# Moving the second layer's cross-attention values out of the decoder's inner loop

## The reference

```python
q = x @ Wq.T + bq                 # 128 x 128, per sequence
k = context @ Wk.T + bk           # 77 x 128
v = context @ Wv.T + bv           # 77 x 128
p = softmax(heads(q) @ heads(k).T)          # 16 heads, each row sums to 1
x = layernorm(x + (p @ heads(v)) @ Wo.T + bo)
```

## Time and profile before

| | us |
|---|---|
| median of 3 runs (lowest, highest) | 801.29 (800.78, 802.55) |
| the profiled execution | 800.58 |
| its span, from first to last instruction | 798.8 |
| busy in the span: PE, PEld, DVE | 662.6, 502.5, 585.7 |
| busy in the span: ACT, POOL | 408.7, 207.4 |
| layer 2, from 478.6 to the end | 320.2 |
| layer 2's loop in its steady part, 516.0 to 750.2 | 234.2 |
| of that PE busy, DVE busy, ACT busy | 212.01, 193.02, 132.25 |

### The profile page before, as it was taken

How to read it: one execution, slowest core, us unless ns; L and a number is a source line. 1 busy time by engine, 2 the same in 40 slices (tenths; PEclk the granted TensorE clock), 3 DMA queues, 4 the chain that set the end, 5 groups by cost and what they waited for, 6 DMA issues and landing times.

```text
span 798.8 us, 20635 instructions
## 1 busy us (share of the span) xinstructions
PE 662.6 (83%) x8166; PEld 502.5 (63%) x8166; DVE 585.7 (73%) x1639; ACT 408.7 (51%) x1172; POOL 207.4 (26%) x212
## 2 busy tenths in 40 slices
PE   5767999999999698998652967889898999989973
PEld 3345777777777476777531965666666666666641
DVE  1346888888888889896746475788888887888743
ACT  3656666666666355664210222465555555565532
POOL 5211233333333311423425042222222222222100
PEclk9969999999999889999955896999999999999975
DMA  9666534445444424450022110000000001100000
GB/s 356 241 198 212 180 124 156 158 164 176 158 159 156 155 57 160 145 213 12 25 86 68 36 39 14 10 12 11 12 12 12 16 12 16 14 12 12 5 5 7
DMA packets 48255, 72.18 MB, mean 90 GB/s; under 512 B 2832, under 2 KB 43280, under 8 KB 45472
## 3 DMA queue, kind: packets, MB, share of 16 engines
q1 hardware_dynamic: 45120, 61.80, 23.0%
q0 software_dynamic: 2320, 5.18, 3.0%
q10 hardware_dynamic: 720, 3.88, 1.2%
HBM read 32.38 MB, written 38.47 MB: 89 GB/s over the span
## 4 chain that ended last, share of the span: by engine, by line
PE 48%; DVE 30%; issue 12%; ACT 6%; DMA 2%; POOL 0%; SPq 0%; DVEq 0%; POOLq 0%; ACTq 0%
PE bank L490 40%; PE bank L542 4%; DVE sc L1172 3%; PE bank L625 3%; DVE nmxa L1176 2%; DVE k L1506 2%; DVE scol L1548 1%; ACT kbd L1094 1%; ACT kbd L1095 1%; DVE q L1226 1%; DVE nmb L1231 1%; DVE k L1484 1%; DVE q L1575 1%; DMA xT_ld<-xT 1%; DVE y_d L1522 1%
## 5 line engine op out<-in xcount | busy, mean ns | idle before, releaser
L431 POOL TENSOR_TENSOR early<-early,recb 128x616 f32<-128x616 f32 x32 | 38.9, 1216 | 212.1 <-DVE recb L1262 212.1
L951 ACT ACTIVATE sc<-sc,nmxa 128x128 f32<-128x128 f32 x256 | 78.1, 389 | 9.6 <-DVE nmxa L1176 9.6
L1506 DVE TENSOR_TENSOR k<-bank,k_sb 128x512 f32<-128x512 f32 x64 | 41.1, 684 | 30.7 <-PE bank L490 20.1
L1172 DVE TENSOR_TENSOR sc<-bank,rel 128x512 f32<-128x512 f32 x64 | 41.1, 683 | 19.1 <-PE bank L490 19.1
L490 PE MATMUL bank<-k,xdT 128*128 128x512 f32 x96 | 49.1, 651 | 0.0
L1184 DVE COPY pTa<-bank 128x512 f32<-128x512 f32 x32 | 21.9, 691 | 33.7 <-PE bank L542 33.6
L490 PE MATMUL bank<-pTb,v 77*32 77x128 f32 x1024 | 37.3, 284 | 10.8 <-DVE pTb L1269 4.9
L408 POOL TENSOR_TENSOR rext<-rext,ones 128x1008 f32<-128x1008 f32 x16 | 29.9, 1868 | 60.3 <-ACT rext L936 60.3
L467 POOL TENSOR_TENSOR oTb<-x_all,row_sb 128x128 f32<-128x128 f32 x16 | 7.6, 478 | 142.9 <-DVE pTa L1527 135.5
L936 ACT ACTIVATE rext<-bank 128x512 f32<-128x512 f32 x64 | 34.8, 608 | 18.1 <-PE bank L490 18.1
L490 PE MATMUL bank<-kbd 32*128 32x256 f32 x256 | 38.1, 417 | 5.3 <-DVE kbd L1500 4.6
(11 more groups left out here) (269 smaller groups left out, 1812.6 us busy)
## 6 DMA issues: line engine op xcount, KB each, us to landing
rel_dram<-rext SPq DMA_DIRECT2D x16, 2040.0 KB, 7.1
rel<-rel_dram SPq DMA_DIRECT2D x16, 960.0 KB, 5.6
rext<-w_up SPq DMA_DIRECT2D x1, 1792.0 KB, 8.3
rel<-w_down SPq DMA_DIRECT2D x1, 1792.0 KB, 8.8
wb<-w_b ACTq DMA_DIRECT2D x1, 1604.0 KB, 16.7
xT_ld<-xT SPq DMA_DIRECT2D x16, 64.0 KB, 7.0
x_all<-x ACTq DMA_DIRECT2D x1, 1024.0 KB, 11.8
rel<-rel_dram SPq DMA_DIRECT2D x16, 64.0 KB, 5.7
```

What stands on the lines that cost most here:

```text
L431: G.tensor_tensor(pB[:, part, :], pB[:, part, :], recb[:, part].unsqueeze(2).broadcast_to([P, 8, C]), ALU.mult).then_inc(b_even, 1)
L951: last = A.activation(sc[:, h, :], sc[:, h, :], ACT.Exp, bias=nmxa[:, h:h + 1])
L1172: added = mark(V.tensor_tensor(sc[:, part[i], :], bank[2 * j + i][:].rearrange("p (a j) -> p a j", a=4), rel[:, t % 2, part[i], :], ALU.add))
L1506: V.tensor_tensor(scd[:, 4 * i:4 * i + 4, :], bank[(1, 2, 0, 1)[i]][:].rearrange("p (a t) -> p a t", a=4), const("causal").unsqueeze(1).br ...
```

## The change

- `v1` leaves both lists of the loop, TensorE's and VectorE's. Between the layers, behind the keys, TensorE makes the values of all 16 sequences into banks 3, 6, 4 and 7, and ScalarE copies them to places in SBUF that are free from then on (seven copies: three of four sequences, four of one).
- A new `v1` on ScalarE copies a sequence's values, SBUF to SBUF, into `ve`, two rounds ahead, between `e_q` and `f_ln`. `e_v` waits for it instead of `e_s`.
- The bias isn't added to the values. VectorE scales the output weights by it (`wo_bv`), TensorE sums that over the features with `ones`, in front of the product with `wabs`, and VectorE adds the row to `c1_bo`.
- The lists are written anew. Read around the ring, the differences are these. TensorE: `e_q` is in front of `f_down` instead of behind it. VectorE: `f_norm` goes from behind `f_i4` to behind `f_clamp`, a round's half later; `c_s1` is in front of `f_q0`; `f_q1`, `f_q2` and `f_q4` are in front of `c_ag`; `f_q3` is in front of `c_norm`; `d_r0` and `d_r1` change places. GpSimd: `d_res` of a sequence runs one round later, in the same place behind `e_res`.

The diff, cut to its core:

```diff
@@ -83,15 +83,15 @@
 ORDER2 = {
-    "pe": ("v1 f_turn:-2 e_out:-1 d_qk:1 e_x d_gv:1 f_down:-2 e_q d_rank:1 f_x:-1 e_s f_up:-1 e_nm d_s01:1 "
-            "e_st d_s3:1 e_inj d_v:1 d_out:1 e_v d_x:2").split(),
-    "dve": ("f_clamp:-1 d_m2:1 d_m3:1 f_silu:-1 c_s0:2 f_q0:-1 c_s1:2 c_st:2 c_ag:2 f_q1:-1 d_add:1 f_q2:-1 "
-            "d_st:1 d_ag:1 c_norm:2 f_q3:-1 f_q4:-1 d_n0:1 d_n1:1 D_st:1 D_ag:1 e_div v1:1 d_norm:1 e_add e_st "
-            "e_ag d_r1:2 e_norm d_r0:2 f_i0 d_rope:2 f_i1 f_add:-1 f_i2 f_st:-1 f_i3 f_ag:-1 f_i4 f_norm:-1 "
-            "d_gate:2 d_q:2 e_m0:1 e_m1:1 e_m2:1 e_m3:1 d_k:2 d_m0:2 d_m1:2").split(),
-    "act": ("e_e2 d_v:1 e_e3 c_ln:2 d_ln:1 e_v d_x:2 d_ln2:1 f_turn:-1 e_ln e_x:1 d_gates:2 e_q:1 f_ln:-1 f_x "
-            "d_sig:2 e_nm:1 f_exp f_sig e_e0:1 e_e1:1").split(),
-    "pool": "gather:2 e_res d_res:2 d_fade:2".split(),
+    "pe": ("d_gv:1 e_q f_down:-2 d_rank:1 f_x:-1 e_s f_up:-1 e_nm d_s01:1 e_st d_s3:1 e_inj d_v:1 d_out:1 e_v "
+            "d_x:2 f_turn:-1 e_out d_qk:2 e_x:1").split(),
+    "dve": ("f_i4:-1 d_gate:1 d_q:1 e_m0 e_m1 e_m2 e_m3 d_k:1 d_m0:1 d_m1:1 f_clamp:-1 f_norm:-2 d_m2:1 d_m3:1 "
+            "f_silu:-1 c_s0:2 c_s1:2 f_q0:-1 c_st:2 f_q1:-1 f_q2:-1 f_q4:-1 c_ag:2 d_add:1 d_st:1 d_ag:1 "
+            "f_q3:-1 c_norm:2 d_n0:1 d_n1:1 D_st:1 D_ag:1 e_div d_norm:1 e_add e_st e_ag d_r0:2 e_norm d_r1:2 "
+            "f_i0 d_rope:2 f_i1 f_add:-1 f_i2 f_st:-1 f_i3 f_ag:-1").split(),
+    "act": ("e_e2 d_v:1 e_e3 c_ln:2 d_ln:1 e_v d_x:2 d_ln2:1 f_turn:-1 e_ln e_x:1 d_gates:2 e_q:1 v1:2 f_ln:-1 "
+            "f_x d_sig:2 e_nm:1 f_exp f_sig e_e0:1 e_e1:1").split(),
+    "pool": "e_res:-1 d_res d_fade:1 gather:2".split(),
     "sp": "f_store:2".split(),
...
@@ -100,6 +100,10 @@
                         "d_r1", "d_rope", "d_rank"), 1)
+V1_BANKS = (3, 6, 4, 7)
...
@@ -248,6 +253,11 @@
         ve, vd = va[0:2], va[2]
+        cflat = cT[:, :, :].rearrange("p b j -> p (b j)")
+        values4 = [cflat[0:C, 0:4 * P], cflat[0:C, 4 * P:8 * P], xT_ld[0:C, :, :].rearrange("p n d -> p (n d)")]
+        values1 = [cflat[0:C, 8 * P:9 * P], y["a"][0:C, :], y["b"][0:C, :], q[2][0:C, :]]
+        v1_sb = [values4[t // 4][:, t % 4 * P:(t % 4 + 1) * P] for t in range(12)] + values1
         nme, nmTe = nmb, nmT
...
@@ -726,14 +736,24 @@
                 mm(bank[i][:, 0:(hi - lo) * C], w("c1_wk"), flat[:, lo * C:hi * C]).then_inc(k0_ps, 1)
+            pe.wait_ge(b_pT_dve, 2 * B)
+            for t in range(B):
+                last = mm(bank[V1_BANKS[t // 4]][0:C, t % 4 * P:(t % 4 + 1) * P], cT[:, t, :], w("c1_wv"))
+                if t % 4 == 3:
+                    last.then_inc(v_ps, 1)
             for n in range(2 * E):
                     pe.wait_ge(k0_sb, 3 * XC + 3)
+                if n == 12:
+                    pe.wait_ge(v_lo, B + 1)
                 last = pe.transpose(bank[n // 4][:, n % 4 * P:(n % 4 + 1) * P], xg[:, n, :], ident)
             pe.wait_ge(w_sum, 1)
+            pe.wait_ge(v_lo, B + 7)
+            mm(bank[7][:, P:2 * P], ones[:], wo_bv[:])
             mm(bank[7][:, 0:2], ones[:], wabs[:]).then_inc(w_mean, 1)
...
@@ -828,7 +848,6 @@
                 need(pe, var["e"], t)
-                pe.wait_ge(v_hi, B + t + 1)
                 for i in range(4):
...
@@ -849,16 +868,13 @@
                 pe.wait_ge(exped["b"], 4 * (B + t) + 4)
+                pe.wait_ge(v_hi, B + t + 1)
                 head_products(bank[3], ve[t % 2], pTe, C)
                 mm(bank[4][:, 0:P], oTe, w("c1_wo")).then_inc(proj["e"], 1)
-            def v1(t):
-                pe.wait_ge(exped["b"], 4 * (B + t))
-                mm(bank[5][0:C, 0:P], cT[:, t, :], w("c1_wv")).then_inc(v_ps, 1)
...
@@ -1052,6 +1068,13 @@
+            for n in range(3):
+                act.wait_ge(v_ps, 2 * B + 4)
+                A.activation(values4[n], bank[V1_BANKS[n]][0:C, :], ACT.Copy).then_inc(v_lo, 1)
+            for n in range(4):
+                A.activation(values1[n], bank[V1_BANKS[3]][0:C, n * P:(n + 1) * P], ACT.Copy).then_inc(v_lo, 1)
             def m_turn(i):
...
@@ -1066,6 +1089,10 @@
                 A.activation(yg[:, n, :], bank[3][:, 0:P], ACT.Copy).then_inc(m_y_act, 1)
+            def v1(t):
+                need(act, values["e"], t - 1)
+                A.activation(heads(ve[t % 2][:])[0:C], by_head(v1_sb[t]), ACT.Copy).then_inc(v_hi, 1)
...
@@ -1410,6 +1437,7 @@
             dve.wait_ge(ld_wf, 16)
+            step(V.tensor_scalar(wo_bv[:], w("c1_wo"), col("c1_bv"), None, ALU.mult))
             step(V.tensor_reduce(wabs[:, 0:1], fw[:, 0:HID], AX.X, ALU.add, apply_absolute_value=True))
...
@@ -1430,6 +1458,7 @@
                 dve.wait_ge(w_mean, 1)
+                V.tensor_tensor(row("c1_bo"), bank[7][:, P:2 * P], row("c1_bo"), ALU.add)
                 V.tensor_scalar(wmean[:], bank[7][:, 0:2], 1.0 / (P * HID), 1e-5, ALU.mult, ALU.max).then_inc(w_ready, 1)
...
@@ -1530,11 +1559,6 @@
                 add("e", 4, lambda t: xe)(t)
-            def v1(t):
-                dve.wait_ge(v_ps, 2 * B + t + 1)
-                V.tensor_tensor(heads(ve[t % 2][:])[0:C], by_head(bank[5][0:C, 0:P]), by_head(row("c1_bv")[0:C, :]),
-                                ALU.add).then_inc(v_hi, 1)
```

33 lines of the change are left out of this document (17 added, 16 removed).

## The result

The changed kernel took 804.22 us (median of 9 runs, 802.87 to 808.02), the kernel before 801.29 (9 runs beside it, 800.78 to 803.36). The ratio is 1.0037, with a 95% interval from 1.0021 to 1.0052: slower by 2.9 us. The forecast was 803.6, with a range of 799.8 to 806.2. Two executions, one of 1101.42 us (kernel before) and one of 1582.3 us (last kernel of the experiments), ran in a far slower state and are left out of every median and ratio.

What follows compares the result with a forecast made beforehand. Each 18.02 us round was bound by TensorE from `d_rank` to the mask, then by VectorE's pace; 0.15 x 13 = 1.95, plus 0.3 between the layers and 0.1 drain, +2.35 on 801.29: 803.6, range 799.8 to 806.2.

Steps and rivals of the forecast that it cites:

- The rule for adding up: On VectorE, an independent follower starts duration - 0.08 later, a dependent one 0.03 after the end; `c_st` to `d_n0` 2.07, +0.11.
- `f_norm`: Moved behind `f_clamp` into VectorE's half of the round: +0.04 per round, at most +0.11, at least 0.
- The sum for the loop: Layer 2's 13 rounds, each longer by 0.04 (`f_norm`) + 0.11 (`f_q` steps) = 0.15: 1.95 us.
- `v1` leaves VectorE: In front of `d_norm`, which waits for ScalarE anyway, removing the 0.28 us step gains 0.00 per round.
- The case of fewer steps: Rival: VectorE's step count sets the second half's pace, `v1` gives 0.20 in 16 rounds: 798.4 us; chance 0.16.
- `v1` enters ScalarE: A copy of about 0.3 between `e_q` and `f_ln`, where ScalarE waits 0.97 for VectorE: 0.00.
- `v1` leaves TensorE: Its 0.38 pair goes, but `e_out` waits 0.32 for VectorE's division, which is late next: 0.00.
- The rival of the clock: Layer 2's start: the hole left by `v1` delays TensorE's clock rise, +1.2 to +3.5, 804.8 to 807.1; chance 0.11.
- GpSimd's sums: Rival: `d_res`, ending 643.3, meets `f_clamp` at 643.41 and holds it 0.2 in 13 rounds: +2.6, 806.2; chance 0.06.
- Between the layers: The product with `ones` comes when TensorE has no slack left: +0.3 (0.2 to 0.6); the values and copies cost 0.
- My sign of being wrong: Wrong if the round is shorter than 18.02, or the stages before 478 us differ by over 1 us.
- The drain: Last rounds, `e_q` in front of `f_down`, where VectorE has less to do ahead of `f_add`: 0.1 once.

Runs made afterwards that it cites:

- last kernel of the experiments: Kernel before with `f_clamp` in front of `d_m0`, `f_exp`, `f_q4`, `f_q1` moved, and `d_v`'s ScalarE copy and GpSimd's gather earlier: 801.79 us beside 802.17, 0.9991.
- the first experiment: Changed kernel with the kernel before's lists, their `v1` taken out (values between the layers, ScalarE's `v1` kept): 801.81 us, 1.0021 to the kernel before.

## Why the prediction was right, and where it wasn't

**The rule for adding up** held. It gave 2.07 for `c_st` to `d_n0`; measured 2.05. The term was +0.11 for a round; the run with the `f_q` steps alone gives 18.10 - 17.99 = +0.11.

**`f_norm`** was +0.04 and is +0.01 (2.99 against 2.98), and the run with it alone shows no longer round. In after `f_silu` starts 647.83 - 646.05 = 1.78 behind `f_clamp`, not 1.81: the step takes 646.63 - 646.38 = 0.25 and not 0.27, and the masks behind it 1.20 and not 1.21. And the earlier trace rows leave `f_silu` a slack of 0.24 and not only the idle 0.16 that I counted with. The sum for the loop, 1.95, should have been 13 x 0.12 = 1.56; the profiled one shows 1.17, because before has one round of 18.31. A single round that is 0.3 longer stands at the same place, the third, in all traces of kernels with `v1` on VectorE (with `f_clamp` alone, in the first three; the two kernels built on that one have a further long round later), and in none with `v1` on ScalarE; of those only the one without the bias row has a longer round, the fifth. The kernel with the product kept on TensorE has none, so the product isn't the cause. Why it is the third round isn't known.

**`v1` leaves VectorE: 0.00.** Right, and shown by the first experiment: `d_norm`'s wait is 0.42, forecast 0.43 to 0.5. The case of fewer steps (798.4) was wrong for this reason.

**`v1` enters ScalarE: 0.00.** Right in the round (17.99 with the old lists). ScalarE's wait in front of `f_ln` shrank from 0.97 to 0.79.

**`v1` leaves TensorE: 0.00 per round**, right for the round, wrong at the start. This is the step of the prediction that failed in the profiled execution: the sum has nothing for the start, and it measured 31.42 against 29.66, +1.76. The rival of the clock, to which I had given 0.11, has the size in its +1.2 to +3.5, but its mechanism is only part of what is seen. It reckoned with a late rise alone and a `d_rank` of up to 1.16 more. The late rise cost 0.53 by the product with `nmb`, and `d_rank` took 1.28 instead of 1.16; the greater part, 1.23, is the second fall, which no rival named. I had seen the hole of some tenths and the earlier trace rows, but not that nearly every kernel which keeps the product has 29.66, which one trace can't show.

**GpSimd's sums** end at 645.50 and `f_clamp` starts at 646.05, so they don't meet. The margin is 0.55 and not 0.1, as `d_fade` comes earlier: 2.63 behind `d_rank` where it was 3.06, so by 0.43 and not by the 0.3 that I had set against it. The last of the three sums:

```profile
645.05 0.45 POOL L478 TENSOR_TENSOR oTb<-x_all,row_sb 128x128 f32<-128x128 f32 x1
```

**Between the layers** +0.3 was forecast, and the product takes 0.43 there. The profiled after starts the experts' first product 1.47 later than before; 0.71 of this are there already at 423 us, where the two kernels do the same, and in layer 2 only 0.37 are left. The product's own delay, about 0.6, was nearer the upper end of my 0.2 to 0.6, but it is made good by layer 2, so as a term of the sum it was 0. (My sign of being wrong, a difference of over 1 us ahead of 478 us, was met at the experts' first product. It doesn't touch layer 2, where 0.37 are left.) One reason why less is left is visible: VectorE's cast at the earlier trace rows took 3.87 us beside GpSimd's product and takes 0.41 in after, where it comes first. The other traces have it both ways: 3.85 to 3.87 in nine of them, 0.41 to 0.48 in three, with and without the changed lists. So I don't credit it to the change.

**The drain** was 0.1 and is +1.17, the second mis-sized term. From the 14th `f_silu` to the last `y_e` it is 25.41 against 25.29, +0.12. That is the size forecast for `e_q` in front of `f_down`, and it isn't shown that `e_q` is the cause: the kernels with `e_q` at its old place and `f_clamp` unmoved have 24.84 to 25.29, those with the new lists 25.38 to 25.74. The rest is one group, the last sequence's products from 786.22. In the chain of what ended last (start, duration, what), before and then after:

```profile
782.80 4.78 PE bank L490 x7
```

```profile
786.22 5.83 PE bank L500 x7
```

5.83 against 4.78, +1.05. The granted clock is at 0.50 until 786 in before, 3.2 us into the group, and 0.96 in the two us behind it; in after it is at 0.50 until 791, 4.8 us into the group, and 0.65 in the us behind that. So more of the seven products run at the lower level. The kernels with a drain of 43.6 to 43.7 all have rounds of 17.93 or 17.99, and every one with another round, longer or shorter, has 44.5 to 45.3. The `f_q` steps alone bring it about (5.73 for that group, drain 44.49), without the move of `e_q`. So the term that I had left out is the level of the clock in the last group; why a round of another length goes with a later rise there each time isn't shown.

**The sum.** In the profiled execution: 0.37 ahead of layer 2, 1.76 at its start, 1.17 in the loop, 1.17 in the drain, 4.47 in all. In the medians 2.9. My 2.35 is near the medians' 2.9 in part by luck. In the profiled execution the loop term was 0.8 too high (0.4 by the median round) and the two ends were too low by 1.8 and 1.1, so the sum was 2.1 too low. That the medians lie nearer to it is because the profiled execution of after is one of its longer ones (805.05 against a median of 804.22) and that of before a shorter one. How the 2.9 of the medians are shared among the four parts isn't known, as each kernel has one profile. The direction and the loop were understood; the ends weren't.

## What to carry to other kernels

Ask of each small step whether it stands in a chain or in a wait: the same 0.2 us operation cost 0.06 us a round in front of `d_n0` and nothing in front of `d_norm`, and a removed operation of 0.28 us in front of a wait gained nothing. The long wait of an engine is the place to look for a step that another engine waits for: one entry of a list moved there (`f_clamp`) made the steady rounds 0.26 us shorter and the whole 1.8 us, as the drain took 1.4 back. Work at the start and the end of a loop, where TensorE is half idle, has to be costed at both levels of its clock. Removing a small product there may cost more than it takes, as the pair of 1.0021 and 0.9994 suggests.

## What the hardware showed that I hadn't expected

- A product that nobody uses made a kernel faster: 1.0021 without it, 0.9994 with it, with the stretch at the start of layer 2 at 31.93 and 29.67. In these traces a wait of 0.37 us ahead of the next products, at the lower level, goes with a rise that comes later. A second fall to 0.50 follows within a few tenths of a us of the end of a wait of 1.71 us. The kernel with the product has the same 1.71 us and doesn't fall.
- That isn't a rule without exceptions: one kernel with the product in its place rose late all the same (four products 1.06, start 32.17), and another rose late and didn't fall again (start 29.83).
- In the drain, the same seven products took 4.78 us in one kernel and 5.83 in the other, at 0.50 for the first 3.2 and 4.8 us of them.
- A VectorE operation of one element per partition (0.12 to 0.21 us by its row) delays an independent follower by only 0.04 to 0.12, and one that stands between two dependent ones by less: `d_add` to `d_ag` is 0.64 with `f_q2` in between the earlier trace rows and 0.62 without it (632.22 to 632.84 in after).
